# The sums and inverse of the attention's denominators are placed earlier in the instruction order of VectorE and TensorE

## The reference

```python
# attention, 16 heads of 16 channels, 6 orders
xq = jnp.clip(q * inv_sqrt_d, -1.0 + EPS_CLAMP, 1.0 - EPS_CLAMP)
xk = jnp.clip(k * inv_sqrt_d, -1.0 + EPS_CLAMP, 1.0 - EPS_CLAMP)
Tq = _cheb(xq)
Tk = _cheb(xk)
Tv = Tk * v[:, :, :, None, :]
kv_prefix = jnp.cumsum(Tv, axis=2)
ks_prefix = jnp.cumsum(Tk.sum(axis=-1), axis=2)
num = (Tq * kv_beta).sum(axis=3)
den = (Tq.sum(axis=-1) * k_beta).sum(axis=3)
out_h = num / (den[..., None] + EPS_DEN)
# routing of the feed-forward part
logits = jnp.einsum('btd,ed->bte', X, routing_W) + expert_bias
activation = jnp.sqrt(jax.nn.softplus(logits))
top_vals, top_idx = jax.lax.top_k(activation, K)
```

## Time and profile before

| | |
|---|---|
| median of 3 runs | 915.92 us (915.1 to 918.37) |
| profiled execution | 915.11 us, span 913.4 us |
| mean granted TensorE clock | 0.968 |
| PE busy | 847.7 us, 93% |
| DVE busy | 798.7 us, 87% |
| ACT busy | 486.2 us, 53% |
| POOL busy | 275.1 us, 30% |

### The profile page before, as it was taken

The page is one execution under the profiler, slowest core; times in us unless marked ns, Lnnn a source line. Parts: engine busy times, 40 slices in busy tenths (PEclk is TensorE's granted clock), DMA queues, the critical chain, the costliest instruction groups (busy, mean ns, idle before and its releaser), DMA issues. The chain is left out here.

```text
span 913.4 us, 14235 instructions
## 1 busy us (share of the span) xinstructions
PE 847.7 (93%) x4377; PEld 645.8 (71%) x4377; DVE 798.7 (87%) x1363; ACT 486.2 (53%) x874; POOL 275.1 (30%) x351
## 2 busy tenths in 40 slices
PE   5784749999999999999999999999999999998998
PEld 5553437786868677886768676877768676866786
DVE  3897969999999989999899989999999999999432
ACT  4753446555656466565656466565656464441321
POOL 1021241423434241423333251523333240413120
PEclk9886859999999999999999999999999999999999
DMA  9022225354544435354534435363635344353431
GB/s 322 2 55 75 47 49 168 71 169 87 152 87 114 129 75 167 70 168 88 149 88 119 125 72 167 71 176 85 167 72 137 76 81 135 78 152 76 122 94 45
DMA packets 51580, 99.98 MB, mean 109 GB/s; under 512 B 5363, under 2 KB 34110, under 8 KB 49478
## 3 DMA queue, kind: packets, MB, share of 16 engines
q1 hardware_dynamic: 36356, 66.14, 22.0%
q0 software_dynamic: 14688, 32.51, 20.5%
q10 hardware_dynamic: 482, 0.74, 0.2%
HBM read 57.68 MB, written 17.06 MB: 82 GB/s over the span
## 5 line engine op out<-in xcount | busy, mean ns | idle before, releaser
L1577 PE MATMUL acc<-w,hid 128*128 128x256 f32 x1128 | 262.6, 380 | 0.3 <-DVE hid L1219 0.3
L1577 PEld LDWEIGHTS acc<-w,hid 128*128 128x128 f32 x1128 | 214.0, 190 | 34.5 <-DVE hid L1219 0.5
L848 ACT ACTIVATE hid<-ring,b1row 128x512 f32<-128x512 f32 x144 | 96.8, 682 | 165.9 <-PE ring L1458 164.5
L673 POOL DMA_DIRECT2D feat<-feat x47 | 42.6, 906 | 344.0 <-DVE feat L1066 210.4
L796 ACT ACTIVATE feat<-ring,bqkv 128x512 f32<-128x512 f32 x96 | 65.9, 687 | 87.4 <-PE ring L1458 87.4
L1219 DVE TENSOR_TENSOR hid<-hid,cfw 128x512 f32<-128x512 f32 x128 | 85.0, 675 | 29.3 <-ACT hid L848 22.0
L1458 PE MATMUL ring<-n2H,w1H 128*128 128x512 f32 x288 | 106.2, 450 | 0.0
L1045 DVE TENSOR_TENSOR_SCAN feat<-zero,carry,feat 128x512 f32<-128x512 f32 x80 | 97.2, 1267 | 0.0
L1045 DVE TENSOR_TENSOR_SCAN feat<-zero,feat 128x512 f32<-128x512 f32 x80 | 92.4, 1205 | 0.0
L1458 PE MATMUL ring<-n2H,w1L 128*128 128x512 f32 x288 | 91.0, 397 | 0.0
L1458 PE MATMUL ring<-n2L,w1H 128*128 128x512 f32 x288 | 91.0, 397 | 0.0
(11 more groups left out here) (169 smaller groups left out, 1397.9 us busy)
## 6 DMA issues: line engine op xcount, KB each, us to landing
feat<-feat POOLq DMA_DIRECT2D x47, 512.0 KB, 4.6
cfw<-cf_rows SPq DMA_DIRECT2D x16, 1280.0 KB, 7.6
xin<-in_L_attn_x SPq DMA_DIRECT2D x16, 512.0 KB, 9.5
feat<-inv_rows SPq DMA_DIRECT2D x32, 256.0 KB
cfw<-cf_rows SPq DMA_DIRECT2D x16, 512.0 KB, 3.6
out<-x SPq DMA_DIRECT2D x15, 512.0 KB, 8.6
out<-fin POOLq DMA_DIRECT2D x15, 512.0 KB, 5.8
cfw<-cf_rows SPq DMA_DIRECT2D x16, 256.0 KB, 4.6
```

The source lines that it names most:

```text
L673: g.dma_start(f(into), f(of), accum_op=ALU.add).then_inc(added[n], 16)
L848: a.activation(hid[:, e % NG], ring[bank][:, :], ACT.Silu, bias=b1row[:, e:e + 1]).then_inc(ring_copied, 1)
L1577: last = mm(acc[t // 2][:, t % 2], hid[:, e % NG, t * P:(t + 1) * P], w2[:, e], start=False, stop=(e == E), skip_group_check=True)
```

## The change

On DVE `logit_parts` is cut in two. `logit_maxima` keeps the sum of the parts, the two maxima and what is made of them; `logit_ranks` has the differences of all pairs and the count. Between them `den_key_sums` and `den_products` of the chunk's attention are issued. The pairs have moved out of the memory of `prod` into that of an order's key feature (`feat[:, KT3, 0]`), which nothing reads any more at this point, and `den_key_sums` no longer waits for the ranks. Behind the ranks comes `invert`, then `clip`, the weighing of expert 5 and `softplus`; before it was the other way round, with `invert` last (in step 1 right behind the clips). In step 0 the order stays. In step 15 the weighing of expert 5 goes ahead of the maxima, that of expert 6 ahead of `softplus`, and those of experts 7 and 8 right behind it.

On PE `denominators` goes from behind `expert(4)` to ahead of it; in step 15 it goes the other way, behind the up product of expert 7 and the down product of expert 5. SyncE, GpSimd and ScalarE keep their order.

The diff, without the new semaphore `maxima_begun` (one increment on DVE that nothing waits for) and the step behind the last attention, where the two new functions stand side by side:

```diff
--- before.py
+++ after.py
@@ -156,7 +156,7 @@
         top = sb("top", [P, NT, 8])
         best = sb("best", [P, 9, NT, K])
         NEG, U, MX, DN, RC, Z, Z2, PL, AC = range(9)
-        pair = prod[:, 0:NT * E * E].rearrange("p (t e j) -> p t e j", t=NT, e=E)
+        pair = feat[:, KT3, 0, 0:NT * E * E].rearrange("p (t e j) -> p t e j", t=NT, e=E)
         part = sb("part", [P, 2, NT, E], bf16)
         rest = sb("rest", [P, NT, E])
         split = sb("split", [P, NT, P // 2])
@@ -1074,7 +1075,6 @@
 
                 c = number(i, p)
                 dve.wait_ge(summed, 2 * c + 1)
-                ge(dve, log_parts, NLOG * c)
                 if p:
                     dve.wait_ge(kcarried, i + 1)
                 v.tensor_tensor_scan(prod[:, :], cv["kshift"].to_broadcast([P, CT]), tr[0][:, :],
@@ -1146,7 +1146,7 @@
                     v.tensor_tensor(x1[:, p, 2 * h:2 * h + 2], tr[h][:, :].rearrange("p (t d) -> p t d", t=2),
                                     xin_of(i, p)[:, 2 * h:2 * h + 2], ALU.add).then_inc(x1_ready, 1)
 
-            def logit_parts(i, p):
+            def logit_maxima(i, p):
 
                 c = number(i, p)
                 at = NLOG * c
@@ -1155,19 +1155,25 @@
                 terms = misc.rearrange("p (t q e) -> p t e q", t=NT, q=P // QS)[:, :, 0:E, 0:LQ // QS]
                 lg = route[:, L_]
                 v.tensor_reduce(lg, terms, AX.X, ALU.add).then_inc(log_parts, 1)
-                others = lg.unsqueeze(2).to_broadcast([P, NT, E, E])
-                own = lg.unsqueeze(3).to_broadcast([P, NT, E, E])
                 dve.wait_ge(log_parts, at + 1)
-                v.tensor_tensor(pair, others, own, ALU.subtract).then_inc(log_parts, 1)
+                dve.sem_inc(maxima_begun, 1)
                 for t in range(NT):
                     last = v.max(top[:, t], lg[:, t])
                 last.then_inc(log_parts, 1)
-                dve.wait_ge(log_parts, at + 3)
+                dve.wait_ge(log_parts, at + 2)
                 best2 = top[:, :, 0:K]
                 v.scalar_tensor_tensor(out=best[:, NEG], in0=best2, scalar=-1.0, in1=best2,
                                        op0=ALU.mult, op1=ALU.min).then_inc(log_parts, 1)
                 v.tensor_scalar(best[:, MX], best2, 0.0, None, ALU.max).then_inc(log_parts, 1)
-                dve.wait_ge(log_parts, at + 2)
+
+            def logit_ranks(i, p):
+
+                at = NLOG * number(i, p)
+                lg = route[:, L_]
+                others = lg.unsqueeze(2).to_broadcast([P, NT, E, E])
+                own = lg.unsqueeze(3).to_broadcast([P, NT, E, E])
+                v.tensor_tensor(pair, others, own, ALU.subtract).then_inc(log_parts, 1)
+                dve.wait_ge(log_parts, at + 5)
                 flatp = pair.rearrange("p t e j -> p t (e j)")
                 v.tensor_tensor(flatp, flatp, tie, ALU.is_ge).then_inc(log_parts, 1)
                 dve.wait_ge(log_parts, at + 6)
@@ -1252,7 +1258,6 @@
                     token_stats(dve, 1, *prev)
                     token_mean_var(dve, 1, *prev)
                 first = isinstance(i, int) and number(i, p) == 0
-                start_up = isinstance(i, int) and number(i, p) <= 1
                 if first:
                     dve.wait_ge(ring_copied, CHUNK0["v1"][0] + 1)
                     weigh(i, p, 0)
@@ -1294,29 +1299,43 @@
                         carry_over(i, p, 1)
                     order_product(i, p, 2)
                     order_product(i, p, 3)
+                last_attention = st is LAST_ATTENTION
+                if last_attention:
+                    expert(5)
                 if second:
-                    logit_parts(*prev)
+                    logit_maxima(*prev)
                 if attn_:
                     den_key_sums(i, p)
                     den_products(i, p)
+                if second:
+                    logit_ranks(*prev)
+                if attn_ and not first:
+                    invert(i, p)
                 if qkv:
                     clip(*nxt, use, 0)
                     clip(*nxt, use, 1)
-                expert(5)
-                if attn_ and start_up:
+                if first:
                     invert(i, p)
+                if not last_attention:
+                    expert(5)
+                else:
+                    expert(6)
                 if second:
                     softplus(*prev)
-                if attn_ and not start_up:
-                    invert(i, p)
-                expert(6)
+                if not last_attention:
+                    expert(6)
+                else:
+                    expert(7)
+                    expert(8)
                 if attn_:
                     prefix(i, p, 4)
-                expert(7)
+                if not last_attention:
+                    expert(7)
                 if attn_:
                     carry_over(i, p, 2)
                     order_product(i, p, 4)
-                expert(8)
+                if not last_attention:
+                    expert(8)
                 if second:
                     combine_weights(*prev)
                 if first:
@@ -1634,9 +1654,9 @@
                 if qkv:
                     project(*nxt, use, "v0")
                     project(*nxt, use, "v1")
-                expert(4)
                 if attn_:
                     denominators(i, p)
+                expert(4)
                 expert(5)
                 expert(6)
                 expert(7)
@@ -1669,10 +1689,11 @@
                 for e in (3, 4):
                     expert_up(*exp, use, e + 2)
                     expert_down(*exp, use, e)
+                expert_up(*exp, use, 7)
+                expert_down(*exp, use, 5)
                 denominators(i, p)
-                for e in (5, 6):
-                    expert_up(*exp, use, e + 2)
-                    expert_down(*exp, use, e)
+                expert_up(*exp, use, 8)
+                expert_down(*exp, use, 6)
                 expert_down(*exp, use, 7)
                 expert_down(*exp, use, 8)
                 expert_up(*prev, after, 0)
```

More of the change, by code:

```diff
@@ L226, in build @@
             [sem(f"norm{n}_{what}") for n in range(2)] for what in ("aggregate_begun", "aggregated", "mean_var", "pow"))
+        maxima_begun = sem("maxima_begun")
         sums_begun, squares_begun, norm_begun = (sem(f"{n}_begun") for n in ("token_sums", "token_squares", "normalisation"))
```

## The result

The changed kernel took a median of **909.68 us** (10 runs, 908.11 to 912.75) beside 916.19 us for the kernel before: ratio 0.9925, 95% interval 0.9908 to 0.9942. It is faster, by 0.75%, but the forecast was 903.2 with a range up to 909: 6.5 us were gained, about half of what was forecast. The profiled execution took 908.4 us where the sum gave 902.8 for it.

The account below looks back on a forecast made before the run. PE was taken as the bound, waiting for DVE's division and products. Gains of 2.3 + 6.7 + 3.3 = 12.3 us took the profiled 915.11 to 902.8, plus 0.4 a forecast median of 903.2, range 900.5 to 909.

Parts of the forecast that it names:

- The step that failed: Behind chunk 15's projection: everything up to the last store shifts with it, leaving the tail at 67.37 us.
- Step 1: Chunk 1's step: inverse write clearly beats the third order sum, division starts at 123.3, a gain of 2.3 us.
- Steps 2 to 14: Middle steps: PE's waits for the division between 150 and 800 us all go, a gain of 6.7 us.
- rival (a): Odd steps and step 15: inverse write loses the race against the third order sum; 908 us, chance 0.2.
- Step 15: Last attention chunk's step: PE's 4.28 us wait for the product shrinks, projection at 842.75, a gain of 3.3 us.
- (b): Race lost in step 1 too, or reads slowed beside the order sum, so nothing comes of it: 912 us, chance 0.06.
- (c): Moved clips hold GpSimd's issue of the order sum, its landing and the numerator come late: 922 us, chance 0.04.
- (d): DVE's new wait ahead of the eps addition costs 0.4 us more in each step: 905.5 us, chance 0.15.
- The sum: Whole kernel: gains of 2.3, 6.7 and 3.3 make 12.3 us, taking the profiled execution from 915.11 to 902.8 us.

Follow-up runs that it names:

- tail_hold: Changed kernel, but GpSimd adds chunk 13's output one step later, once the last combine weights' first two slices have landed: 904.18 us.
- before_again: The kernel before, run and profiled once more without any edit: 915.67 us.
- hold_in_before: The kernel before, with only the addition of chunk 13's output held until the last combine weights' first two slices have landed: 917.55 us, ratio 1.0002.
- after_again: The changed kernel, run and profiled once more without any edit: 908.32 us.
- behind_write: Changed kernel, with the addition of chunk 13's output held only until the small write of the last combine weights has landed: 908.16 us.
- lose_race: Changed kernel, but SyncE's write of the inverses waits for GpSimd's mark of the third order sum, set ahead of its issue: 909.19 us.
- clips_first: Changed kernel with the two clips ahead of the inverse again on DVE, behind the ranks: 912.87 us.
- late_inverse: Changed kernel with DVE's inverse back behind softplus in steps 2 to 15, behind the clips in step 1; expert 6 moved in step 15: 918.00 us.
- old_last: Changed kernel with chunk 15's step back in its old order on PE and DVE: 911.30 us.
- late_dens: Changed kernel with PE's denominators behind expert 4 again, DVE and step 15 as changed: 949.83 us.
- old_last_hold: Changed kernel with chunk 15's step in its old order and chunk 13's addition held until the last combine weights' first two slices landed: 910.10 us.

## Why the prediction was wrong, point by point

**The step that failed** is the last of the working: "Everything behind it, up to the last store, hangs on this projection by PE's order and shifts with it." The tail hangs on two things that shift by different amounts. The projection of chunk 15 came 3.3 us sooner against what is ahead of it by the forecast (2.75 measured), because it stops waiting for `den_products`. The addition of chunk 13's output hangs on DVE behind the division, which the same paragraph moved by less than half of that (842.77 to 841.3). Before, the division was 3.26 us ahead of the projection; after, 1.40. The missing 1.86 is what the addition comes later against the projection (from -0.11 to +1.77), and the write of the last combine weights stands a fixed 4.7 to 4.8 us behind the projection (850.74 - 846.03, 840.37 - 835.56). Its margin before was small: the addition landed at 851.6 and the write's reads went out at 852.24. Both DMAs stood in the trace of before, and it was the same pattern as the race of the earlier trace rows: a small write behind a large addition ends with it. I looked for it at the one place the change aims at, and not where the two chains meet next. It cost 3.8 us; tail_hold gives 3.4 to 3.7 of them back, and lands at 904.2, where the forecast had 903.2. A smaller part of the miss is the size of step 1's term.

**Step 1** (2.3 forecast): 2.2 by the first pair of profiles, 0.4 by the second. The mechanism came as forecast: write 0.76 us ahead of the sum, reads 1.96 us later. The size didn't. GpSimd's third sum of this step is issued either 37.1 to 37.4 or 38.0 to 38.7 us behind chunk 0's projection, whatever the order; the first pair had 38.01 before and 37.15 after, and 0.86 of its 2.2 us is that chance. Counted from the sum's issue, the projection starts after 11.95, 11.93 and 11.30 us in the three profiles of the old order (before, before_again, hold_in_before), and after 10.5 to 10.7 us in after, after_again, tail_hold, behind_write and lose_race: 1.1 us in the mean. Most of the missing 1.2 us is the division. It was put at 123.3, 8.3 us behind the sum's issue at 115.04, and stands 9.0 to 9.3 behind it, because in the changed kernel the sum, with the reads now beside it, landed after 5.3 us and not 4.8 (4.7 in clips_first, where the reads come behind it), and the division came 3.8 us behind that landing.

**Steps 2 to 14** (6.7): 7.24 and 5.7, 6.5 in the mean of all profiles, waits down from 6.7 to 0.2. Right, with the mechanism confirmed by late_inverse (all lost again) and clips_first (3.1 lost, when the write falls 0.2 to 0.65 us behind the sum; 3.4 are left, near the 3.3 that rival (a) gave for a lost race). One reading was off: the lone write's packets in the earlier trace rows fall in the slices 66.5 to 66.9, which is 1.3 to 1.7 us after its issue at 65.20 and not 1.5 to 1.9, so the margin was 0.2 us wider than I had it.

**Step 15** (3.3): 2.75 and 3.5, 3.2 in the mean. The wait of 4.28 is 0.58, no low clock follows it, and waits of 0.48, 0.41 and 0.66 came up, for the weighed tiles and the division; old_last puts the whole at 2.6.

**The rivals.** (a), the lost race: not in the changed kernel; the write won in step 13 and 15 with 0.37 and 0.16 us, and clips_first shows its price. (b): fell. (c), the clips hold GpSimd's DMA: the third sums of steps 3 to 14 land after 4.9 to 5.0 us, 0.3 us later than before at most. The Trainium skill, "SBUF — State Buffer", SBUF: two separate sides, gives 0.62 us grown to 3.1 us for a DMA of GpSimd beside a VectorE copy. Here the overlap is there, and nothing of the 2.5 us is seen in those steps; the one third sum of 7.4 us, in step 2, whose cause no run looked for, cost DVE 0.3 us. The price of (c) was also added up wrong: 902.8 + 21 is 923.8, not 922. (d), a dearer wait on DVE: 0.4 us at most, 1.9 in all between 150 and 800 us; late_dens shows how steep that would have been.

**The sum.** Between 902.8 and the profiled 908.4 are 5.6 us: 3.8 of the tail, 1.7 of the start-up and 0.1 of the rest. As an account of this one pair that is right, but the 1.7 is chance and so is the 0.1. By the means of all profiles in which nothing between the projections differs (three of the old order, five of the new), 0.85 + 6.5 + 3.2 = 10.5 us were won there, 1.8 less than forecast. The tail took 3.9 of them (71.3 against 67.4), which leaves 6.6; the medians differ by 6.5.

**The tail, over all runs.** The kernels that were made for the race tell it too. By the time between the projection of chunk 15 and the issue of the addition:

| addition issued | kernels | reads issued | PE's wait | clock behind it | tail |
|---|---|---|---|---|---|
| -0.69, -0.11 | before_again, before | +6.21 | 0.47, 0.25 | full | 67.6, 67.4 |
| +0.41 | old_last | +6.79 | 1.25 | fell | 70.0 |
| +1.23 | late_inverse | +7.34 | 1.76 | full | 68.9 |
| +1.76 to +1.77 | after, after_again, lose_race, clips_first, late_dens | +8.04 to +8.30 | 2.31 to 2.59 | fell | 71.1 to 71.4 |
| +8.33 to +14.22 | behind_write, tail_hold, hold_in_before, old_last_hold | +6.19 to +6.30 | 0.21 to 0.88 | full | 67.3 to 68.0 |

In the three middle rows the reads come at the addition's landing or up to 0.3 us behind it, and PE's wait grows with them. Two numbers then make up every tail: without PE's wait it is 67.1 to 67.2 us in the seven kernels whose clock stayed full, and 68.7 to 68.9 in the six whose clock fell. So the lower clock is a second price of some 1.7 us that is paid or not: behind 1.25 us it was, behind 1.76 not.

## What to carry to other kernels

When a change pulls one chain forward, write down by how much each of the neighbouring chains moves, and follow them to the next place where they meet, above all where their DMAs share the engines: what stays in step with its neighbour is safe, what moves by another amount is a new race. A small DMA on which an engine will wait should be issued ahead of a large one (here 0.15 us were enough); where its issuer can't be made earlier, hold the large one, if nobody waits for it. Time by cuts at a marker that every version has, and take more than one profile of each: here the start-up scatters by 4 us and step 1 by over 1, as much as most terms of the sum.

## What the runs showed of the hardware

- A small write (32 KB) issued 0.2 to 0.65 us behind a 512 KB accumulating DMA of GpSimd took 4.3 to 4.9 us until the reads that wait for it (clips_first; 4.65 in step 1 before), and 2.0 us when it was issued 0.03 us or more ahead, but for steps 5 and 14 of the changed kernel (3.03 and 2.86 us) and step 14 of lose_race (2.62). The write of the combine weights, issued 3.0 us behind an addition, took 3.2 to 3.5 us, against 1.5 us alone. The reads of the late writes came from 0 to 0.9 us behind the sum's or addition's landing.
- Reads issued 2.03 us ahead of such an addition were hardly slowed by it: the first slice (256 KB) landed 4.3 us behind its issue in behind_write and in tail_hold, the second (1280 KB) 7.4 against 7.0 us. The addition itself landed 8.5 us after its issue there and 10.0 in tail_hold, against 5.7 before; nobody waits for it.
- A wait of PE of 2.31 us, and one of 1.25, was followed by a lower granted clock (0.61 over 849 to 853 us in the changed kernel, of the two levels the 1.2 GHz one for most of it) and cost 1.7 us more than its own length; behind one of 1.76 us, and behind all of 0.21 to 0.88 us in the same place, the clock stayed at 1.00. Nor does PE's work just ahead sort them: in the 4 us before the wait ended it was busy for 2.17 us in old_last, where the clock fell, and for 1.64 us in late_inverse, where it didn't. What decides it stays open.
- The time to the first projection scatters between 77.0 and 81.2 us over the profiles, whatever the order. Why stays open; no run here was made for it.
